# Three pairs of tiles in seven block products instead of two, the first pair's right columns computed last, and the x sums of the second pair made early

## The chip, the cores and the metric

The kernel runs on one core of one Trainium2 chip. The metric is device time in microseconds (us), the median of several executions. One of the executions is recorded by the hardware profiler, and all rows below come from that one. Engines are named as in the profile: PE is TensorE, PEld its weight load, DVE is VectorE, ACT is ScalarE, POOL is GpSimd, SP is SyncE. A small q (SPq, POOLq) means the engine's sequencer: what it does itself, such as issuing DMAs or loading registers.

## The reference

Eight tiles of 128 tokens by 512 features go through a dense layer with one low-rank adapter chosen for each tile, then through a second dense layer with a top-2 gate over eight rank-16 experts. The result is added to x.

```python
A = lora_A[adapter_indices]; Bm = lora_B[adapter_indices]
h = einsum('bsi,io->bso', x, W) + einsum('bsr,bro->bso', einsum('bsi,bir->bsr', x, A), Bm)
result = einsum('bnd,od->bno', h, W_base) + b_base
probs = softmax(einsum('bnd,ed->bne', h, W_gate)); top_p, top_i = top_k(probs, 2)
route_w = sum(one_hot(top_i, E) * (top_p / sum(top_p))[..., None])
delta = einsum('bner,eor->bno', einsum('bnd,erd->bner', h, A_exp) * route_w[..., None], B_exp)
out = x + result + delta
```

## The kernel before

**Fold.** Both dense layers are linear in x, so W is first multiplied into the gate's, the experts' and W_base's columns. This gives one matrix of 648 columns in four row chunks of 128: a left part (8 gate columns, 128 expert columns, 256 output columns, kept in cl_hi and cl_lo with 16 adapter columns beside it, 408 together) and a right part (the other 256 output columns, cr_hi and cr_lo). The identity is added so that x itself comes out too.

**Split in two.** Every fp32 operand is kept as a rounded part (hi) and the remainder (lo), and a `product` (L679 to L682) is three matmuls: hi by hi, hi by lo, lo by hi. ACT makes most hi parts, DVE makes most lo parts by a subtraction (helper `lo`, L500), POOL makes some of both.

**Tiles.** The eight tiles are four pairs q = 0 to 3. Pairs 0 and 3 are computed plainly: `Left(t)` is four products of 408 columns and `Right(t)` four of 256. Pairs 1 and 2 are computed with seven block products (Q1 to Q7, each two chunks deep) in place of eight. Q1, Q2, Q4 and Q5 have 408 columns, Q3, Q6 and Q7 have 256. Q3, Q5, Q6 and Q7 take sums of the two tiles of x, made on POOL by `x_sums` (L324) and split by `split_sums`; Q4 and Q5 take differences of blocks of the folded matrix (u_hi, u_lo), Q6 and Q7 others (v_hi, v_lo), made on DVE and split by ACT and DVE. Between the seven products DVE adds partial results (`sum_v`, `sum_w`, `sum_d`).

**Around the products of a pair.** `split_xa` (DVE) takes the adapter columns out of PSUM, T1 (PE) transposes them, ACT copies them out (`copy_xa_t`), `Lora_left` and `Lora_right` (PE) add the adapter's contribution with rows of bw_rows. bw_rows is filled by DMAs (`spread`) from bw_hi and bw_lo. Then `gate(q)` (DVE, L586) finds the two best experts and writes hw, T2 (PE) transposes hw, ACT and DVE split it (`split_hw`), and `Delta(t)` (PE) adds the experts' part to the left and right output. ACT or DVE copies the outputs to y_out, SP stores them.

**Order.** Each engine's program is one list written by hand, with semaphores between engines. The order of PE is the list from L888 on. POOL's order is: read the adapter numbers into registers (L272), eight DMAs for the adapters' weights (L275), identity and zero fills, the bias rows and their four DMAs (L303), adapter columns of tiles 0 and 1 (`split_la`), then x sums and the rest. SP issues all other loads, then the 24 DMAs of `spread`, then the stores.

Of the kernel before, what the change touches and what calls it, by code (L numbers as in the profile page):

```python
# [5 lines left out]
F32 = mybir.dt.float32  # L6
# [6 lines left out]
NT = 8  # L13
# [13 lines left out]
SEVEN = 2  # L27
LA_ORDER = (0, 1, 2, 3, 4, 5, 6, 7)
# [13 lines left out]
def adaln_ffn_kernel(nc, x_t, itok, fold_in, lora, ffn_b, bias, out):  # L42
    ctx = ExitStack()
    with ctx:
# [3 lines left out]
        def sem(name):  # L48
# [7 lines left out]
        ffn_b_raw = sb("ffn_b_raw", [P, D])  # L56
        bias_raw = sb("bias_raw", [1, D])
# [33 lines left out]
        s_hi, s_lo = (half[:].rearrange("p (n a) (b c x) -> p n (a b) c x", n=SEVEN, b=2, c=2) for half in (wt_hi, wt_lo))  # L91
# [4 lines left out]
        xa_t = sb("xa_t", [P, 2, P], F32R)  # L96
# [21 lines left out]
        left_bank = [(bank[0], bank[1]), (bank[5], bank[2])]  # L118
        right_bank = [(bank[6], bank[7]), (bank[4], bank[3])]
# [18 lines left out]
        last_left_copied = sem("last_left_copied")  # L138
        even_zeros, odd_zeros = sem("even_zeros"), sem("odd_zeros")
        bw_loaded = [sem(f"bw_loaded{q}") for q in range(PAIRS)]  # L140
        bias_rows_loaded = sem("bias_rows_loaded")
# [4 lines left out]
            sem("la_diff_done"), sem("s_summed"), sem("s_hi_done"), sem("s_lo_done"), sem("x_tail_lo_done"))  # L146
        q1_done, q5_done, q6_done, q7_done, q1_copied, v_done, w_done, d_done, yc_done = (
# [38 lines left out]
        def at_front(t):  # L186
            return t in (0, 2, 3, 6)
# [13 lines left out]
        def right(t):  # L201
            return right_whole(t)[:, 0:HALF]

        def t1_out(q):
            return right_whole(2 * q)[:, HALF:HALF + P]

        def t2_out(q):
            return left(4)[:, 0:2 * P] if q == PAIRS - 1 else right_whole(2 * q + 1)[:, HALF:HALF + 2 * P]

        def wait_right_copied(engine, t):  # L210
            if t // 2 in (1, 2):
                engine.wait_ge(yc_done, t - 1)
            else:
                engine.wait_ge(yr_done, t + 1 if t < 2 else t - 3)
# [11 lines left out]

        def sync_program(sp):
# [12 lines left out]
            sp.dma_start(bias_raw[:], bias).then_inc(bias_loaded, DMA)  # L240

            sp.wait_ge(lora_loaded, NT * DMA)
            for t in range(2, NT):
                load_x(t)

            def spread(part, n, q, loaded):
                for h in range(2):
                    sp.dma_start(bw_rows[h * Q + n * R:h * Q + (n + 1) * R, h, q, :].bitcast(F32),
                                 part[h * Q + q * R:h * Q + (q + 1) * R, :].bitcast(F32)).then_inc(loaded, DMA)
# [12 lines left out]

            for t in range(NT - 1):
                sp.wait_ge(yl_done, t + 1)
                wait_right_copied(sp, t)
                sp.dma_start(out[t], y_out[:, t]).then_inc(out_stored, DMA)
            sp.wait_ge(last_left_copied, 1)
            sp.dma_start(out[NT - 1, :, HALF:], y_left(NT - 1)).then_inc(out_stored, DMA)
            sp.wait_ge(out_stored, (NT + 1) * DMA)

        def gpsimd_program(pool):
            _, adapters = nc.values_load_multi_w_load_instructions(  # L272
                itok[0:1, :], engines=[mybir.EngineType.Pool], min_val=0, max_val=NA - 1)
            for b in range(NT):
# [6 lines left out]
            nc.gpsimd.iota(expert_id[:], pattern=[[1, E]], base=0, channel_multiplier=0,  # L281
                           allow_small_or_imprecise_dtypes=True).then_inc(const_ready, 1)

            nc.gpsimd.memset(xa_rows[:].bitcast(F32), 0.0).then_inc(const_ready, 1)
            pool.wait_ge(const_ready, 2)
            for h in range(2):
                nc.gpsimd.memset(xa_rows[:, :, h * Q + ONES:h * Q + ROWS].bitcast(F32), 1.0).then_inc(const_ready, 1)
            pool.wait_ge(const_ready, 4)
            pool.wait_ge(ident_ready, 1)
            nc.gpsimd.tensor_copy(ident_r[:], ident[:]).then_inc(ident_ready, 1)  # L290
            nc.gpsimd.memset(bw_rows[:, 1].bitcast(F32), 0.0).then_inc(odd_zeros, 1)
            pool.wait_ge(odd_zeros, 1)
            pool.wait_ge(even_zeros, 1)

            pool.wait_ge(bias_loaded, DMA)
            nc.gpsimd.tensor_copy(bias_hi[:], bias_raw[:]).then_inc(bias_hi_done, 1)
            pool.wait_ge(bias_hi_done, 1)
            nc.gpsimd.tensor_tensor(bias_lo[:], bias_raw[:], bias_hi[:].bitcast(F32), ALU.subtract).then_inc(bias_lo_done, 1)
            pool.wait_ge(bias_lo_done, 1)
            for h in range(2):  # L300
                for n, part in enumerate((bias_hi, bias_lo)):
                    row = h * Q + ONES + n
                    pool.dma_start(bw_rows[row:row + 1, h, :, GH:].bitcast(F32),  # L303
                                   part[:].bitcast(F32).unsqueeze(1).broadcast_to([1, PAIRS, D])).then_inc(bias_rows_loaded, DMA)

            pool.wait_ge(lora_loaded, NT * DMA)

            def split_la(t):
                n = LA_ORDER.index(t)
                odd = t in (3, 5)  # L310
                if t in (2, 4, 6, 7):
                    pool.wait_ge(left_done, {2: 1, 4: 2, 6: 3, 7: 5}[t])
# [11 lines left out]
            def x_sums(q):  # L324
                n = q - 1
                a, b = x_raw[:, 2 * q], x_raw[:, 2 * q + 1]
                pool.wait_ge(cl_lo_done, 1)
                pool.wait_ge(x_loaded[2 * q], DMA)
                pool.wait_ge(x_loaded[2 * q + 1], DMA)
                nc.gpsimd.tensor_tensor(s_raw[n][0][:, 0], b[:, 0:2], b[:, 2:4], ALU.add).then_inc(s_summed, 1)  # L330
                pool.wait_ge(s_summed, 4 * n + 1)
                nc.gpsimd.tensor_tensor(s_raw[n][0][:, 1], s_raw[n][0][:, 0], a[:, 0:2], ALU.add).then_inc(s_summed, 1)
                pool.wait_ge(s_summed, 4 * n + 2)
                nc.gpsimd.tensor_tensor(s_raw[n][1][:, 0], s_raw[n][0][:, 1], a[:, 2:4], ALU.add).then_inc(s_summed, 1)
                nc.gpsimd.tensor_tensor(s_raw[n][1][:, 1], a[:, 0:2], b[:, 0:2], ALU.add).then_inc(s_summed, 1)

            def split_sums(q, h):
# [15 lines left out]
            split_sums(2, 0)  # L353
            split_la(4)
            split_la(5)
            split_sums(2, 1)
            pool.wait_ge(hw_done, 4)
            for t in (NT - 2, NT - 1):
                pool.wait_ge(x_hi_done, t + 1)
                nc.gpsimd.tensor_tensor(x_lo[:, t], x_raw[:, t], x_hi[:, t].bitcast(F32), ALU.subtract).then_inc(x_tail_lo_done, 1)  # L360
            split_la(6)
            split_la(7)

        def scalar_program(act):
# [14 lines left out]
            def split_x(t):  # L379
                chunks = slice(2, KC) if t in (3, 5) else slice(0, KC)  # L380
# [3 lines left out]
            split_x(0)  # L384
            split_x(1)
# [3 lines left out]
            act.wait_ge(ffn_b_loaded, DMA)  # L389
            nc.scalar.copy(ffn_b_hi[:], ffn_b_raw[:]).then_inc(ffn_b_hi_done, 1)  # L390
# [6 lines left out]
            for n in range(2):  # L397
                act.wait_ge(cr_summed, n + 1)
                if n == 0:
                    act.wait_ge(cr_plus_i, 1)  # L400
                nc.scalar.copy(cr_hi[:, 2 * n:2 * n + 2, :].rearrange("p c n -> p (c n)"), bank[4 + n][:]).then_inc(cr_hi_done, 1)
# [584 lines left out]
```

## Time and profile before

| what | value |
|---|---|
| runs | 64.83, 65.61 and 66.38 us, median 65.61 us |
| profiled execution, its own time | 64.86 us |
| its span, first to last instruction | 63.6 us |
| PE busy | 59.8 us, 94% of the span |
| DVE, POOL, ACT busy | 42.0, 31.5, 29.9 us |
| granted TensorE clock | 1.000 throughout |

A row of the timeline gives the start, the duration, engine, line, operation, output and inputs, and how often it stands in the row. PE's matmuls are pipelined: the step from the start of one to the start of the next is what one costs, the duration also holds the way through the array. A bracket gives the idle time just before a row and what ended it.

### The profile page before, as it was taken

How to read it: one execution, taken by the hardware profiler on the slowest of the kernel's cores; microseconds unless marked ns; L12 is line 12 of the kernel's file. 1: busy time of each engine (PE TensorE's matmuls, PEld its weight loads, DVE VectorE, ACT ScalarE, POOL GpSimd, SP SyncE). 2: the span in 40 equal slices, each digit the busy share in tenths (PEclk: the TensorE clock that was granted, in tenths of full speed). 3: DMA queues.
4: the chain of work that ended last, by engine and by line, in shares of the span. 5: the costliest groups of instructions: out<-in, count | busy, mean ns of one | idle time of the engine just before them, and what ended most of it. 6: DMA issues, size and time to landing. Idle time of an engine off the chain costs nothing.

```text
span 63.6 us, 1254 instructions
## 1 busy us (share of the span) xinstructions
PE 59.8 (94%) x406; PEld 58.8 (92%) x406; DVE 42.0 (66%) x129; ACT 29.9 (47%) x69; POOL 31.5 (49%) x58
## 2 busy tenths in 40 slices
PE   4979999999999999999999999999999999999930
PEld 4969999999999999999999999999999999999820
DVE  0948799918089789999798489089373774195220
ACT  1753999334349869777455014580224102422240
POOL 1000799899969899999865891005960000000000
PEclk9999999999999999999999999999999999999999
DMA  0799999506796000323232323171003400000827
GB/s 0 195 394 345 378 391 406 205 15 184 254 315 255 7 0 0 72 59 72 59 73 62 75 55 84 28 271 67 0 0 148 182 0 10 0 0 13 317 90 240
DMA packets 5048, 8.46 MB, mean 133 GB/s; under 512 B 1057, under 2 KB 1569, under 8 KB 5042
## 3 DMA queue, kind: packets, MB, share of 16 engines
q1 hardware_dynamic: 4370, 7.57, 36.5%
q0 software_dynamic: 384, 0.56, 2.5%
q10 hardware_dynamic: 288, 0.27, 1.2%
q8 instruction: 3, 0.05, 0.3%
q14 instruction: 3, 0.02, 0.1%
HBM read 5.26 MB, written 2.10 MB: 116 GB/s over the span
## 4 chain that ended last, share of the span: by engine, by line
PE 90%; DMA 5%; ACT 1%; issue 0%
PE bank L680 22%; PE bank L682 21%; PE bank L681 21%; PE bank L688 8%; PE bank L690 6%; DMA w_raw<-fold_in 5%; PE bank L843 3%; PE bank L805 2%; PE bank L813 1%; PE bank L847 1%; PE bank L822 1%; ACT y_out L446 1%; PE bank L858 1%; PE bank L854 1%; PE bank L794 0%
## 5 line engine op out<-in xcount | busy, mean ns | idle before, releaser
L680 PE MATMUL bank<-cl_hi,x_hi 128*128 128x408 f32 x24 | 8.5, 356 | 0.0
L682 PE MATMUL bank<-cl_hi,x_lo 128*128 128x408 f32 x24 | 8.4, 348 | 0.0
L681 PE MATMUL bank<-cl_lo,x_hi 128*128 128x408 f32 x24 | 8.3, 348 | 0.0
L275 POOL DMA_DIRECT2D lora_raw<-lora x8 | 4.5, 564 | 6.4 <-issue 6.2
L341 POOL TENSOR_TENSOR wt_lo<-w_raw,wt_hi 128x512 fp32r<-128x512 f32 x4 | 5.5, 1383 | 1.6 <-DVE hw L605 1.3
L438 ACT CAST hw_hi<-bank 128x256 fp32r<-128x256 f32 x4 | 1.5, 373 | 9.1 <-PE bank L822 9.1
L442 ACT COPY y_out<-bank 128x256 f32<-128x256 f32 x7 | 2.6, 374 | 5.3 <-PE bank L682 5.2
L360 POOL TENSOR_TENSOR x_lo<-x_raw,x_hi 128x512 fp32r<-128x512 f32 x2 | 2.5, 1294 | 5.1 <-DVE hw L605 5.1
L501 DVE TENSOR_TENSOR x_lo<-x_raw,x_hi 128x512 fp32r<-128x512 f32 (+1 forms) x6 | 4.9, 834 | 0.0
L680 PE MATMUL bank<-ffn_b_hi,hw_hi 128*128 128x256 f32 x16 | 4.8, 297 | 0.0
L680 PE MATMUL bank<-cr_hi,x_hi 128*128 128x256 f32 x16 | 4.6, 290 | 0.0
L681 PE MATMUL bank<-ffn_b_lo,hw_hi 128*128 128x256 f32 x16 | 4.5, 284 | 0.0
L681 PEld LDWEIGHTS bank<-cl_lo,x_hi 128*128 128x128 f32 x24 | 4.5, 189 | 0.0
L680 PEld LDWEIGHTS bank<-cl_hi,x_hi 128*128 128x128 f32 x24 | 4.5, 188 | 0.0
L682 PE MATMUL bank<-ffn_b_hi,hw_lo 128*128 128x256 f32 x16 | 4.5, 282 | 0.0
L681 PE MATMUL bank<-cr_lo,x_hi 128*128 128x256 f32 x16 | 4.5, 282 | 0.0
L682 PE MATMUL bank<-cr_hi,x_lo 128*128 128x256 f32 x16 | 4.5, 282 | 0.0
L682 PEld LDWEIGHTS bank<-cl_hi,x_lo 128*128 128x128 f32 x24 | 4.5, 188 | 0.0
L382 ACT CAST x_hi<-x_raw 128x512 fp32r<-128x512 f32 (+1 forms) x8 | 4.2, 566 | 0.0
L680 PE MATMUL bank<-wg_hi,wt_hi 128*128 128x392 f32 (+2 forms) x12 | 3.9, 326 | 0.0
L681 PE MATMUL bank<-wg_lo,wt_hi 128*128 128x392 f32 (+2 forms) x12 | 3.9, 324 | 0.0
L682 PE MATMUL bank<-wg_hi,wt_lo 128*128 128x392 f32 (+2 forms) x12 | 3.9, 324 | 0.0
(151 smaller groups left out, 197.3 us busy)
## 6 DMA issues: line engine op xcount, KB each, us to landing
x_raw<-x_t SPq DMA_DIRECT2D x8, 256.0 KB, 4.6
out<-y_out SPq DMA_DIRECT2D x7, 256.0 KB, 2.1
w_raw<-fold_in SPq DMA_DIRECT2D x4, 256.0 KB, 4.7
w_raw<-fold_in SPq DMA_DIRECT2D x3, 324.0 KB, 4.8
bw_rows<-bw_hi SPq DMA_DIRECT2D x16, 40.5 KB, 2.0
lora_raw<-lora POOLq DMA_DIRECT2D x8, 64.0 KB, 3.2
bw_rows<-bw_lo SPq DMA_DIRECT2D x8, 40.5 KB, 2.1
ffn_b_raw<-ffn_b SPq DMA_DIRECT2D x1, 256.0 KB, 6.0
```

The costliest lines, as they stand in the source:

```text
L275: pool.dma_start(lora_raw[:, b, :], lora[bass.ds(adapters[b], 1), :, :].rearrange("a p c -> (a p) c")).then_inc(lora_loaded, DMA)
L341: nc.gpsimd.tensor_tensor(s_lo[:, n, two], s_raw[n][h], s_hi[:, n, two].bitcast(F32), ALU.subtract).then_inc(s_lo_done, 1)
L360: nc.gpsimd.tensor_tensor(x_lo[:, t], x_raw[:, t], x_hi[:, t].bitcast(F32), ALU.subtract).then_inc(x_tail_lo_done, 1)
L382: nc.scalar.copy(x_hi[:, t, chunks], x_raw[:, t, chunks]).then_inc(x_hi_done, 1)
L442: nc.scalar.copy(y_left(t), left(t)[:, OUT_LEFT]).then_inc(yl_done, 1)
L501: nc.vector.tensor_tensor(out, raw, hi.bitcast(F32), ALU.subtract).then_inc(done, 1)
L680: nc.tensor.matmul(out, a_hi, b_hi, start=first, stop=False, skip_group_check=True)
L681: nc.tensor.matmul(out, a_hi, b_lo, start=False, stop=False, skip_group_check=True)
L682: return nc.tensor.matmul(out, a_lo, b_hi, start=False, stop=last, skip_group_check=True)
L688: nc.tensor.matmul(bank[i][:, cols], w[:, m, rows], wg[:, m, cols], start=False, stop=False, skip_group_check=True)
L690: nc.tensor.matmul(fold_right(i), w[:, m, rows], wg[:, m, LEFT:], start=False, stop=False, skip_group_check=True)
L843: nc.tensor.matmul(bank[i][:, 0:GH], w_raw[:, 0, i * P:(i + 1) * P], raw_gh(0), start=True, stop=False, skip_group_check=True)
```

## The change

Pair 3 is computed with Q1 to Q7 as well. The right columns of tiles 0 and 1 (`Right(0)`, `Right(1)`) leave the beginning of PE's tile list and stand behind pair 3's delta, with `Lora_right(0)` and the right deltas of tiles 0 and 1; both results share one PSUM bank and leave by one copy and one store. `Delta` is divided into a left and a right part. Left banks of tiles 2, 3 and the right bank of tile 1's old place are exchanged (PSUM banks 2, 5, 7).

The x sums of pair 1 move on POOL from behind the adapter columns to in front of them, right behind the identity, with their own tiles s_first; their lo part moves from POOL to DVE. POOL now also makes ffn_b_lo, cr_lo of the last two chunks, and the x sums of pair 3. The four bias DMAs move from POOL to SP. The two DMAs of bw_lo for pair 0 move from SP to POOL. POOL's two long fills (bw_rows, xa_rows) move in front of the register loads. SP loads x of tiles 2 and 3 before ffn_b. On DVE the lo parts of v stand in front of the adapter columns of tiles 0 and 1. At the end ACT stores the left half of tile 7 and SP the right half.

```diff
-            load_x(0)
-            load_x(1)
-            sp.dma_start(ffn_b_raw[:], ffn_b).then_inc(ffn_b_loaded, DMA)
+            for t in range(4):
+                load_x(t)
...
             sp.wait_ge(lora_loaded, NT * DMA)
+            sp.dma_start(ffn_b_raw, ffn_b).then_inc(ffn_b_loaded, DMA)
...
         def gpsimd_program(pool):
+            nc.gpsimd.memset(bw_rows[:, 1].bitcast(F32), 0.0).then_inc(odd_zeros, 1)
+            nc.gpsimd.memset(xa_rows[:].bitcast(F32), 0.0).then_inc(const_ready, 1)
             _, adapters = nc.values_load_multi_w_load_instructions(
...
+            x_sums(1)
+            nc.gpsimd.iota(expert_id[:], pattern=[[1, E]], base=0, channel_multiplier=0,
...
             split_la(0)
             split_la(1)
-            x_sums(1)
...
+            pool.wait_ge(ffn_b_hi_done, 1)
+            nc.gpsimd.tensor_tensor(ffn_b_lo[:], ffn_b_raw, ffn_b_hi[:].bitcast(F32), ALU.subtract).then_inc(ffn_b_lo_done, 1)
             x_sums(2)
+            pool.wait_ge(cr_tail_hi_done, 1)
+            nc.gpsimd.tensor_tensor(cr_lo[:, 2:4], cr_raw, cr_hi[:, 2:4].bitcast(F32), ALU.subtract).then_inc(cr_tail_lo_done, 1)
+            pool.wait_ge(bw_lo_done, 2)
+            pool.wait_ge(even_zeros, 1)
+            pool.wait_ge(odd_zeros, 1)
+            spread(pool, bw_lo, 1, 0, first_bw_lo_loaded)
             split_la(2)
-            split_sums(1, 0)
             split_la(3)
-            split_sums(1, 1)
+            x_sums(3)
             pool.wait_ge(hw_done, 2)
...
+            for h in range(2):
+                dve.wait_ge(s_hi_done, h + 1)
+                two = slice(2 * h, 2 * h + 2)
+                lo(s_part(1, 1)[:, two], s_raw[0][h], s_part(0, 1)[:, two], first_s_lo_done)
...
-            ALL = (0, 1, 2, 3)
-            Left(0, ALL)
-            Left(1, ALL)
-            Right(0, ALL)
+            Left(0)
+            Left(1)
+            Q6(1)
             T1(0)
-            Right(1, ALL)
+            Q1(1)
             Lora_left(0)
-            Lora_right(0)
-
-            Q1(1)
-            Q6(1)
             Q5(1)
             Q7(1)
             Q2(1)
             T2(0)
+            Q3(1)
             Q4(1)
-            Q3(1)
-            Delta(0)
-            Delta(1)
+            Delta_left(0)
+            Delta_left(1)
             T1(1)
...
-            Left(6, (0, 1))
+            Q1(3)
             Lora_left(2)
-            Left(6, (2, 3))
-            Left(7, (0, 1, 2))
+            Q6(3)
+            Lora_right(2)
+            Q5(3)
+            Q7(3)
+            Q2(3)
             T2(2)
-            Left(7, (3,))
-            Q3(2)
-            Lora_right(2)
+            Q4(3)
+            Q3(3)
             T1(3)
-            Delta(4)
+            Delta_left(4)
+            Delta_right(4)
             Lora_left(3)
-            Delta(5)
-            Right(6, ALL)
-            Right(7, (0, 1))
+            Delta_left(5)
+            Delta_right(5)
+            Right(0, (0, 1, 2, 3))
+            Right(1, (0, 1))
             T2(3)
-            Right(7, (2, 3))
+            Right(1, (2, 3))
+            Lora_right(0)
+            Delta_right(0)
+            Delta_right(1)
             Lora_right(3)
-            Delta(6)
-            Delta(7)
+            for t in (6, 7):
+                Delta_left(t)
+                Delta_right(t)
```

## Rows read from the trace of the kernel before

**Rows 1.** The page, busy time of each engine and its share of the span.
```profile
PE 59.8 (94%) x406; PEld 58.8 (92%) x406; DVE 42.0 (66%) x129; ACT 29.9 (47%) x69; POOL 31.5 (49%) x58
```
**Rows 2.** Busy time by stretch: length, PE, PEld, DVE, ACT, POOL, clock, DMA.
```profile
27.73:39.60 11.87, 11.87 (x87) 11.82 (x87) 10.11 (x32) 5.67 (x15) 8.65 (x15) 1.00 0.31 67
61.10:63.60 2.50, 0.00 (x0) 0.00 (x0) 0.05 (x1) 0.36 (x1) 0.00 (x0) 1.00 0.60 210
```
**Rows 3.** The page, the chain that ended last, shares of the span by engine.
```profile
PE 90%; DMA 5%; ACT 1%; issue 0%
```
**Rows 4.** Timeline of PE, from Lora_left(0) to Delta(0).
```profile
30.69 0.52 PE L805 MATMUL bank<-bw_rows,xa_t 114*128 114x392 f32 x2
31.05 0.41 PE L813 MATMUL bank<-bw_rows,xa_t 114*128 114x256 f32 x2
31.30 0.35 PE L680 MATMUL bank<-cl_hi,x_hi 128*128 128x408 f32 x1
...
32.42 0.28 PE L680 MATMUL bank<-v_hi,wt_hi 128*128 128x256 f32 x1
...
37.40 0.28 PE L680 MATMUL bank<-cr_hi,wt_hi 128*128 128x256 f32 x1
...
38.11 0.28 PE L680 MATMUL bank<-ffn_b_hi,hw_hi 128*128 128x256 f32 x1
```
**Rows 5.** Timeline of PE, the last Lora_right and the first matmul of Delta(6).
```profile
58.98 0.40 PE L813 MATMUL bank<-bw_rows,xa_t 114*128 114x256 f32 x2
59.35 0.38 PE L680 MATMUL bank<-ffn_b_hi,hw_hi 128*128 128x256 f32 x1
```
**Rows 6.** Timeline of ACT and of DVE, the last copies to y_out.
```profile
61.09 0.37 ACT L446 COPY y_out<-bank 128x256 f32<-128x256 f32 x1 [0.34 <-PE bank L682]
...
60.73 0.42 DVE L676 COPY y_out<-bank 128x256 f32<-128x256 f32 x1 [1.43 <-PE bank L682]
```
**Rows 7.** Timeline of POOL: set-up, bias, adapter columns, x sums, a lo part.
```profile
12.29 0.13 POOL L281 IOTA expert_id<- 128x8 f32 x1
...
13.16 2.27 POOL L291 MEMSET bw_rows<- 128x2592 f32 x1
...
17.90 0.52 POOL L303 DMA_DIRECT2D bw_rows<-bias_hi  x1 [0.29 <-POOL bias_lo L298]
...
20.24 0.25 POOL L318 CAST cl_hi<-lora_raw 128x64 fp32r<-128x64 f32 x1
...
21.68 0.74 POOL L330 TENSOR_TENSOR w_raw<-x_raw 128x256 f32<-128x256 f32 x1
...
24.72 0.73 POOL L330 TENSOR_TENSOR w_raw<-x_raw 128x256 f32<-128x256 f32 x1
25.53 1.13 POOL L332 TENSOR_TENSOR w_raw<-w_raw,x_raw 128x256 f32<-128x256 f32 x1
...
31.56 1.30 POOL L341 TENSOR_TENSOR wt_lo<-w_raw,wt_hi 128x512 fp32r<-128x512 f32 x1
```
**Rows 8.** Timeline of DVE: a lo part of x, gate(0), its sums, gate(1)'s onehot.
```profile
25.38 0.68 DVE L501 TENSOR_TENSOR x_lo<-x_raw,x_hi 128x512 fp32r<-128x512 f32 x1
...
31.25 0.17 DVE L588 MAX8 top_val<-bank 128x8 f32<-128x8 f32 x1 [0.31 <-PE bank L805]
...
32.02 0.88 DVE L594 TENSOR_TENSOR onehot<-expert_id,top_idx 128x32 f32<-128x32 f32 x1
...
33.51 0.61 DVE L605 SCALAR_TENSOR_TENSOR hw<-bank,top_rcp,route 128x128 f32<-128x128 f32 x2
...
35.15 0.43 DVE L622 TENSOR_TENSOR bank<-bank,w_raw 128x256 f32<-128x256 f32 x1 [0.21 <-PE bank L682]
...
42.11 0.19 DVE L594 TENSOR_TENSOR onehot<-expert_id,top_idx 128x32 f32<-128x32 f32 x1
```
**Rows 9.** POOL's sequencer: the loads of the adapter numbers (duration, first and last start).
```profile
L272 POOLq TENSOR_LOAD <-itok x1: 2412/2412/2412, 1.7 to 1.7; - x1
```
**Rows 10.** The page, DMA issues: KB each, us from issue to landing.
```profile
ffn_b_raw<-ffn_b SPq DMA_DIRECT2D x1, 256.0 KB, 6.0
```

More of the change, by code:

```diff
@@ L225, in adaln_ffn_kernel, with spread @@
         LORA_LEFT = slice(R, OWN)
+        def spread(engine, part, n, q, loaded):
+            for h in range(2):
+                engine.dma_start(bw_rows[h * Q + n * R:h * Q + (n + 1) * R, h, q, :].bitcast(F32),
+                                 part[h * Q + q * R:h * Q + (q + 1) * R, :].bitcast(F32)).then_inc(loaded, DMA)
         def sync_program(sp):
@@ L244, in sync_program @@
+            for t in range(4, NT):
                 load_x(t)
[L246 to L249, printed above, removed]
             sp.wait_ge(even_zeros, 1)
             sp.wait_ge(odd_zeros, 1)
+            sp.wait_ge(bias_lo_done, 1)
+            for h in range(2):
+                for n, part in enumerate((bias_hi, bias_lo)):
+                    row = h * Q + ONES + n
+                    sp.dma_start(bw_rows[row:row + 1, h, :, GH:].bitcast(F32),
+                                 part[:].bitcast(F32).unsqueeze(1).broadcast_to([1, PAIRS, D])).then_inc(bias_rows_loaded, DMA)
@@ L263, in sync_program @@
-            for t in range(NT - 1):
+                spread(sp, bw_hi, 0, q, bw_loaded[q])
+                spread(sp, bw_hi, 2, q, bw_loaded[q])
+                spread(sp, bw_lo, 1, q, bw_loaded[q])
+            sp.wait_ge(yl_done, 2)
+            sp.dma_start(out[0:2, :, HALF:].rearrange("t p d -> p t d"), y_out[:, 0:2, HALF:]).then_inc(out_stored, DMA)
+            for t in range(2, 6):
                 sp.wait_ge(yl_done, t + 1)
-                wait_right_copied(sp, t)
+                sp.wait_ge(yc_done, t - 1)
@@ L280, in gpsimd_program @@
                                     pattern=[[-1, P]], channel_multiplier=1).then_inc(ident_ready, 1)
[L281 to L306, printed above, removed]
             def split_la(t):
                 n = LA_ORDER.index(t)
-                odd = t in (3, 5)
+                odd = t in (3, 5, 7)
                 if t in (2, 4, 6, 7):
-                    pool.wait_ge(left_done, {2: 1, 4: 2, 6: 3, 7: 5}[t])
+                    pool.wait_ge(left_done, {2: 1, 4: 2, 6: 3, 7: 4}[t])
                 hi, lo = (u_hi, u_lo) if odd else (cl_hi, cl_lo)
@@ L396, in scalar_program @@
                 nc.scalar.copy(cl_hi[:, i, LORA_LEFT], bank[i][:, 0:LEFT]).then_inc(cl_hi_done, 1)
[L397 to L401, printed above, removed]
+                if i == 1:
+                    act.wait_ge(ffn_b_loaded, DMA)
+                    nc.scalar.copy(ffn_b_hi[:], ffn_b_raw).then_inc(ffn_b_hi_done, 1)
+            act.wait_ge(cr_plus_i, 1)
+            nc.scalar.copy(cr_hi[:, 0:2, :].rearrange("p c n -> p (c n)"), bank[4][:]).then_inc(cr_hi_done, 1)
             for i in range(2):
@@ L523, in vector_program @@
                 lo(lb(lb_lo, h), raw_lb(h), lb(lb_hi, h), lb_lo_done)
-            dve.wait_ge(ffn_b_hi_done, 1)
-            lo(ffn_b_lo[:], ffn_b_raw[:], ffn_b_hi[:], ffn_b_lo_done)
+            for h in range(2):
+                dve.wait_ge(s_hi_done, h + 1)
+                two = slice(2 * h, 2 * h + 2)
+                lo(s_part(1, 1)[:, two], s_raw[0][h], s_part(0, 1)[:, two], first_s_lo_done)
             def split_left(i):
@@ L549, in vector_program @@
             split_left(3)
-            for n in range(2):
-                split_right(n)
+            dve.wait_ge(cr_hi_done, 1)
+            lo(cr_lo[:, 0:2, :].rearrange("p c n -> p (c n)"), bank[4][:], cr_hi[:, 0:2, :].rearrange("p c n -> p (c n)"), cr_lo_done)
             dve.wait_ge(c_raw_done, 3)
@@ L673, in vector_program @@
             split_hw(3)
[L675 to L676 removed]
+            out_right(6)
+            out_right(7)
         def tensor_program(pe):
```

320 lines of the change are left out of this document (173 added, 147 removed).

## Prediction

> **What bounds the kernel now.** I read the page's busy table first: PE has 59.8 us of 63.6, nearly its whole span, and POOL, which this change loads more, 31.5 [rows 1]. The chain that ended last is 90% PE and 5% DMA, the loads before PE's first matmul and the last store [rows 3]. So PE is not only busy, it is the chain. The stretches then say whether it ever waits: from 27.73, where Right(0) begins, to 39.60 it is busy 11.87 us of 11.87, and in the last 2.50 us it does nothing, as only copies and stores are left [rows 2]. Two things can therefore move the end: the number of matmuls, or a wait that PE does not have today. The timelines of the other engines show how early each of PE's inputs is ready.
>
> **What PE saves.** Plain pair 3 takes 8 products of 408 columns and 8 of 256. In seven products it takes 8 of 408 (Q1, Q2, Q4, Q5, two chunks each) and 6 of 256. Two products of 256 go, six matmuls. Q3(1) is six such matmuls and takes 38.11 - 37.40 = 0.71 us [rows 4]. All other work on PE keeps its count. So -0.7.
>
> A small wait goes too. The last Lora_right ends its issue at 58.98 + 0.24, but Delta(6) starts at 59.35 and its first matmul takes 0.38 us instead of 0.28, as hw_lo has only just come [rows 5, 4]. After the change 1.9 us of matmuls that need nothing of gate 3 stand between T2(3) and that delta (half of Right(1), two Lora_right, two right deltas: 6 + 2 + 6 + 2 matmuls at about 0.12). So -0.2. Together -0.9.
>
> **The end.** Before, the last copy is ACT's, 0.37 us from 61.09; now it is DVE's out_right, and a DVE copy of that size took 0.42 [rows 6]. The last stretch stays DMA-bound at a busy share of 0.60 [rows 2]. The store of the first pair's right halves falls in front of it, but can be issued some 1.0 us before PE ends (Lora_right(3) and the last deltas are 14 matmuls, 1.7 us, less the copy). I take 0, bounds -0.1 and +0.4.
>
> **What moves to the front on PE.** Right(0) and Right(1) covered 24 matmuls, 2.9 us, between the fold and pair 1. Everything that pair 1 needs is due that much earlier. Steps: a Q of 408 columns costs 32.42 - 31.30 = 1.12, one of 256 costs 0.71, Lora_left 0.36 [rows 4]. Left(1) still ends at 27.73. Then Q6(1) to 28.44, T1(0), Q1(1) from 28.5 to 29.6, Lora_left(0) at 29.6 (before: 30.69), Q5, Q7, Q2, and T2(0) at 32.9.
>
> **POOL, in front of Q1(1).** Q1(1) needs tile 2's adapter columns, split_la(2), now the end of a long POOL list. It starts when x of tile 3 has landed: ffn_b, issued third behind x, took 6.0 us and would be in by about 11.8 [rows 10]; x of tile 3 comes one transfer of 256 KB later, about 12.4 (estimate). Prices [rows 7]: x_sums 24.72 - 21.68 = 3.04, twice; the small set-up 13.16 - 12.29 less the fill that left, 0.6; split_la (21.68 - 20.24)/2 = 0.72, three times; bias from 15.43 (end of the fill) to 17.90, 2.4; ffn_b_lo and the rest of cr_lo 1.30 each; two DMA issues (20.24 - 17.90)/2 = 1.2. Sum 15.0, so split_la(2) ends at 27.4, and Q1(1) wants it at 28.5. 1.1 us to spare, if nothing slows POOL.
>
> Something does. At 25.53 an x sum took 1.13 us instead of 0.74, beside a DVE subtraction with both inputs in SBUF from 25.38 to 26.06: 0.39 lost [rows 7, 8]. Before the change the x sums of pair 1 had no such neighbours. Now seven DVE subtractions of this kind come beside POOL's list: x of tiles 2 and 3, the two lb_lo, the two lo parts of the first x sums, and the first of v. None hitting costs 0, all cost 2.7; I take half, 1.35, as each can also be the one that waits. POOL then ends at 28.75 and Q1(1) waits 0.25 (bounds 0 and 1.6). bw_lo's DMAs, moved to POOL's queue just ahead, are issued 0.72 before split_la(2) ends and due at Lora_left(0), 1.1 behind Q1(1)'s start; these 1.8 us cover the transfer, and without that cover it adds to the same wait. The wait for bw_lo on POOL is over by then; queued behind it are split_la(2), split_la(3) and x_sums(3).
>
> The Trainium skill, page "SBUF — State Buffer", section "SBUF: two separate sides", gives a rule for this: DVE, with two SBUF inputs, and a POOL instruction reading SBUF take an exclusive lock, and the loser waits for the whole instruction. The rows agree in kind (0.39 of 0.68 lost after a start 0.15 later). By the rule all seven meetings would cost in full; that is the second rival.
>
> **DVE, in front of T2(0).** gate(0) started 0.56 us after Lora_left(0) and had hw at 34.12, 2.87 later. Of this 0.69 is a meeting: onehot took 0.88 and ended at 32.90, beside a POOL subtraction from 31.56 to 32.86; gate(1)'s took 0.19 [rows 4, 7, 8]. Free, hw comes 0.56 + 2.18 = 2.74 after Lora_left(0), and T2(0) now wants it after 3.29 (0.36 + 1.12 + 0.71 + 1.12): 0.55 to spare. sum_d ends 1.46 after hw (35.58 - 34.12), 0.21 of that a wait, so at 3.99, and Q4(1) wants it at 4.2 (T2 about 0.2 and Q3 0.71 later): 0.2 to spare. But x_sums(3) now stands on POOL just there: from about 29.8 to 32.8 (split_la(3) about 1.0, then 3.04) against gate(0) at 30.4. I take one meeting at the row's price, 0.69, less the 0.2: 0.5. Bounds 0 and 1.3 (gate held until x_sums(3) is over).
>
> **Edits that I cost at nothing.** POOL's fills in front of the register loads: the loads run on POOL's sequencer (2.4 us for the numbers alone) while the engine idles [rows 9], so 2.6 us of fill hide there; without that cover see the third rival. The bias DMAs on SP stand in its wait for bw_hi. The two DMAs fewer of pair 0 bring all later spreads forward. v's lo parts stand in front on DVE, where the lo parts of x 2 and 3 stood; I count them as in time for Q6(1) at 27.7, and if they are late, that goes into the same 0.25 and its bounds, since Q1(1) stands right behind. The exchanged banks and new slots add waits that are long met. T1(1), T1(3) and Q1(2) have only about 0.1 to 0.2 us to spare; whatever delays DVE shows there next.
>
> **Sum.** -0.7 - 0.2 + 0.25 + 0.5 = -0.15. On the profiled execution's own 64.86 us this gives 64.7. That execution stands 0.75 under the median of the runs, near the lowest; a median should come at 65.61 - 0.15 = 65.5 us.
>
> **Rivals.**
> - *POOL keeps up.* Meetings on POOL cost under 1.1 and gate(0) slips between the x sums. Then no new wait: -0.9, 64.7 as a median. For it: 1.1 us of slack, and that each meeting has two possible losers. Against: onehot's 0.88. Chance 0.33.
> - *POOL late in full, slower than before.* All seven meetings cost 0.39: split_la(2) ends at 30.1, Q1(1) waits 1.6; x_sums(3) runs to 34.2 and holds gate(0) until then; from the end of onehot hw took 34.12 - 32.90 = 1.2, so hw is at 35.4 against 33.95 free, 1.45 late, 1.25 behind the slack of Q4. 2.85 - 0.9 = +1.95, median 67.55. It decides for "slower" as soon as both waits pass 2.2. For it: POOL and DVE are both nearly full in that stretch (8.65 and 10.11 us of 11.87 even before [rows 2]). Against: in the rows not every meeting cost POOL. Chance 0.20.
> - *The fills delay the register loads.* If POOL's sequencer waited for its engine, the adapter DMAs and all of POOL's list come 2.6 us later: Q1(1) waits 2.85, net +2.45, median 68.05. Against: nothing is waited for between fill and loads. Chance 0.06.
>
> The forecast, a part of the saving eaten by one or both waits, has 0.37; its own range is 64.9 to 66.6 (net -0.7 to +1.0). 0.04 is left for a wait that I have not seen.
>
> **Range.** The first rival, at 64.7 with 0.4 for the spread of the runs, sets the low end, 64.3; the second, half of it, the high end, 67.3. About 2% is what a measurement of this kernel can tell from no change: 64.3 and 66.9. Faster by more needs 1.3 us, and only 0.9 is to be saved, so 0.05 (spread alone). Slower: most of the second rival, the third, a little of the rest, 0.25. Within: 0.70.
>
> **What would show it.** PE's busy time falls by about 0.7 and its idle time shows a wait in front of Q1(1) put down to POOL's split_la(2) (L320), and one in front of T2(0) or Q4(1) put down to DVE. x_sums rows above 0.74 us beside DVE's lo rows confirm the meetings; gate(0)'s onehot or top_diff above 0.2 the second wait. The adapter DMAs on POOL must not start later than before. The prediction is wrong if PE has no idle time (first rival), if the adapter DMAs start some 2.6 us later (third), or if the end is not 2.5 us after PE's last matmul.

## The result, and the profile after

The changed kernel takes 65.95 us in the median, the kernel before 64.77 in the runs beside it. The ratio is 1.020, with a 95% interval of 1.0155 to 1.0242. So the change makes the kernel about 2% slower, at least 1.5% by the interval. Ratios compare runs in the faster of the two states that executions fall into, so they can differ from the ratio of two medians. I had forecast a net of -0.15 us, next to no change. The profiled execution takes 65.83 us with a span of 64.6, which is 1.0 more than before, at a granted clock of 1.00 throughout.

First the page of the changed kernel: the busy table, and of the chain that ended last the shares by engine.

```profile
PE 59.8 (92%) x400; PEld 58.1 (90%) x400; DVE 44.4 (69%) x133; ACT 30.8 (48%) x70; POOL 36.9 (57%) x63
...
PE 84%; DVE 5%; DMA 5%; issue 2%
```

Six matmuls are gone (400 for 406 in [rows 1]), and still PE is as long busy as before. The reason comes below: a short wait in front of a matmul is covered by the listed duration of the matmul before it, and so shows as busy time. The chain was 90% PE [rows 3]. Now it is 84%, and DVE stands in it with 5%, where it did not appear before. POOL has 5.4 us more to do.

Next the busy time by stretch of the changed kernel (length, then PE, PEld, DVE, ACT, POOL, clock, DMA).

```profile
27.73:36.00 8.27, 7.24 (x42) 6.21 (x42) 6.63 (x25) 4.12 (x10) 6.61 (x13) 1.00 0.34 76
36.00:45.00 9.00, 9.00 (x60) 8.94 (x60) 5.49 (x25) 2.67 (x8) 6.42 (x11) 1.00 0.20 55
...
62.00:64.60 2.60, 0.00 (x0) 0.00 (x0) 0.42 (x1) 0.05 (x1) 0.00 (x0) 1.00 0.83 290
```

Before, PE was busy every moment from 27.73 to 39.60 [rows 2]. Now it loses 1.03 us of busy time in the first 8.27 us and nothing from 36 to 45. The last stretch is about as long as before (2.60 for 2.50), and fuller of transfers (0.83 for 0.60). The timeline of PE in the changed kernel shows the places.

```profile
28.25 0.26 PE L817 MATMUL bank<-ident_r,xa_rows 128*114 128x128 f32 x1
29.18 0.42 PE L704 MATMUL bank<-cl_hi,x_hi 128*128 128x408 f32 x1 [0.66 <-issue]
...
30.36 0.54 PE L829 MATMUL bank<-bw_rows,xa_t 114*128 114x392 f32 x2
...
33.48 0.34 PE L706 MATMUL bank<-cl_hi,x_lo 128*128 128x408 f32 x1
34.09 0.59 PE L844 MATMUL bank<-ident,hw 128*128 128x128 f32 x2 [0.26 <-DVE hw L628]
34.67 0.39 PE L704 MATMUL bank<-cr_hi,s_first_hi 128*128 128x256 f32 x1
...
35.38 0.28 PE L706 MATMUL bank<-cr_hi,s_first_lo 128*128 128x256 f32 x1
35.76 0.43 PE L704 MATMUL bank<-wg_hi,x_hi 128*128 128x408 f32 x1
```

Read the starts, not the durations. T1(0) starts at 28.25 and Q1(1) only at 29.18; where nothing waits that step is 0.10, so 0.83 is lost. The last matmul of Q2 starts at 33.48 and costs 0.19, so T2(0) was due at 33.67. It starts at 34.09, and Q3 behind it starts 0.58 later, where that step takes 0.13 in a kernel without the wait: T2's second transpose waits for its own half of hw, and Q3 waits for DVE's next sum, `sum_v`. Q4(1) starts 0.38 behind the last matmul of Q3 instead of 0.11; it waits for the last of these sums, `sum_d`. The bracket in front of Q1(1) names no releaser ("issue"); what it waited for is seen in POOL's timeline of the changed kernel.

```profile
12.95 1.07 POOL L335 TENSOR_TENSOR w_raw<-x_raw 128x256 f32<-128x256 f32 x1 [0.67 <-DMA x_raw<-x_t]
14.09 0.80 POOL L337 TENSOR_TENSOR w_raw<-w_raw,x_raw 128x256 f32<-128x256 f32 x1
...
16.94 0.68 POOL L363 CAST ident_r<-ident 128x128 fp32r<-128x128 f32 x1
17.57 0.70 POOL L318 CAST cl_hi<-lora_raw 128x64 fp32r<-128x64 f32 x1
...
25.00 1.20 POOL L340 TENSOR_TENSOR w_raw<-x_raw 128x256 f32<-128x256 f32 x1
...
28.76 0.32 POOL L320 TENSOR_TENSOR cl_lo<-lora_raw,cl_hi 128x64 fp32r<-128x64 f32 x1
...
31.01 0.73 POOL L337 TENSOR_TENSOR w_raw<-w_raw,x_raw 128x256 f32<-128x256 f32 x1
31.83 0.74 POOL L339 TENSOR_TENSOR w_raw<-w_raw,x_raw 128x256 f32<-128x256 f32 x1
32.52 0.74 POOL L340 TENSOR_TENSOR w_raw<-x_raw 128x256 f32<-128x256 f32 x1
```

split_la(2) ends at 29.08, and Q1(1) starts 0.10 later. The x sums that took 0.74 in [rows 7] take up to 1.20. Then gate(0), `sum_v` (L635) and `sum_d` (L645) in DVE's timeline of the changed kernel.

```profile
31.22 0.55 DVE L613 TENSOR_TENSOR top_diff<-top_val 128x4 f32<-128x4 f32 x1
...
32.09 0.52 DVE L617 TENSOR_TENSOR onehot<-expert_id,top_idx 128x32 f32<-128x32 f32 x1
32.64 0.63 DVE L620 TENSOR_TENSOR top_sum<-top_exp 128x2 f32<-128x2 f32 x1
...
33.68 0.61 DVE L628 SCALAR_TENSOR_TENSOR hw<-bank,top_rcp,route 128x128 f32<-128x128 f32 x2
34.20 0.41 DVE L635 TENSOR_TENSOR w_raw<-bank,w_raw 128x256 f32<-128x256 f32 x1
...
35.18 0.43 DVE L645 TENSOR_TENSOR bank<-bank,w_raw 128x256 f32<-128x256 f32 x1
```

Three subtractions and sums on a handful of elements take 0.52 to 0.63. gate(1)'s onehot took 0.19 [rows 8]. Set the two fences side by side: top_diff ends at 31.77 and the x sum beside it at 31.74; onehot at 32.61 and 32.57; top_sum at 33.27 and 33.26. Each DVE instruction ends as soon as the POOL instruction that was running when it began is over. The row of before that the prediction leaned on shows the same: onehot ended at 32.90, the POOL subtraction beside it at 32.86 [rows 7, 8].

The Trainium skill, page "SBUF — State Buffer", section "SBUF: two separate sides", states such a lock: a DVE instruction with two SBUF inputs and a GpSimd instruction that reads SBUF exclude each other for a whole instruction, and the one that starts first goes first. These three pairs of ends agree with it within 0.04 us. The 0.16 to 0.19 us that these instructions take when nothing holds them do not come on top.

### The profile page after: what moved, and what is told of

It reads as the page before. It is cut to its first block, busy times and chain, and to the rows that moved or that the text cites. A ratio compares the mean times of both kernels' runs of the same rounds, so it can differ in the third digit from the quotient of the medians.

```text
span 64.6 us, 1257 instructions
## 1 busy us (share of the span) xinstructions
PE 59.8 (92%) x400; PEld 58.1 (90%) x400; DVE 44.4 (69%) x133; ACT 30.8 (48%) x70; POOL 36.9 (57%) x63
## 4 chain that ended last, share of the span: by engine, by line
PE 84%; DVE 5%; DMA 5%; issue 2%
PE bank L704 21%; PE bank L706 19%; PE bank L705 19%; PE bank L712 8%; PE bank L714 5%; DMA w_raw<-fold_in 5%; PE bank L869 3%; PE bank L829 2%; PE bank L844 2%; PE bank L835 1%; PE bank L873 1%; DVE top_sum L620 1%; DVE top_diff L613 1%; DVE onehot L617 1%; DVE y_out L649 1%
## 5 line engine op out<-in xcount | busy, mean ns | idle before, releaser
L704 PE MATMUL bank<-cl_hi,x_hi 128*128 128x408 f32 x20 | 7.1, 354 | 0.7 <-issue 0.7
L705 PE MATMUL bank<-cl_lo,x_hi 128*128 128x408 f32 x20 | 7.0, 348 | 0.0
L706 PE MATMUL bank<-cl_hi,x_lo 128*128 128x408 f32 x20 | 7.0, 348 | 0.0
L704 PEld LDWEIGHTS bank<-cl_hi,x_hi 128*128 128x128 f32 x20 | 3.8, 188 | 0.8 <-issue 0.8
L649 DVE TENSOR_TENSOR y_out<-bank,w_raw 128x256 f32<-128x256 f32 x6 | 2.4, 421 | 2.7 <-PE bank L706 2.7
L526 DVE TENSOR_TENSOR x_lo<-x_raw,x_hi 128x512 fp32r<-128x512 f32 (+1 forms) x6 | 3.9, 709 | 0.0
L705 PEld LDWEIGHTS bank<-cl_lo,x_hi 128*128 128x128 f32 x20 | 3.8, 188 | 0.0
L706 PEld LDWEIGHTS bank<-cl_hi,x_lo 128*128 128x128 f32 x20 | 3.8, 188 | 0.0
L402 ACT CAST wt_hi<-w_raw 128x512 fp32r<-128x512 f32 x4 | 2.5, 620 | 2.6 <-DMA w_raw<-fold_in 2.4
L863 PE MATMUL bank<-const-bfloat16-1.0 128*128 128x128 bf16 x24 | 2.7, 309 | 0.9 <-PEq L1011 0.9
```

The costliest lines, as they stand in the source:

```text
L526: nc.vector.tensor_tensor(out, raw, hi.bitcast(F32), ALU.subtract).then_inc(done, 1)
L649: nc.vector.tensor_tensor(y_right(t), right(t), w_sum[:, (t // 2 - 1) % 2], ALU.add if t % 2 else ALU.subtract).then_inc(yc_done, 1)
L704: nc.tensor.matmul(out, a_hi, b_hi, start=first, stop=False, skip_group_check=True)
L705: nc.tensor.matmul(out, a_hi, b_lo, start=False, stop=False, skip_group_check=True)
L706: return nc.tensor.matmul(out, a_lo, b_hi, start=False, stop=last, skip_group_check=True)
L863: nc.tensor.matmul(bwr_bank[:, 0:P], ones, ones, start=True, stop=True)
```

## The experiments

The theory after this reading: the saving on PE is there in full, and two waits eat it, both made of meetings between POOL instructions and DVE subtractions. Runs are compared with the kernel before on the same chip. Start times vary between executions even for the same code (in the traces below the fold begins between 5.58 and 7.45), so beside the medians I use the distance from the first split matmul of the fold to the last matmul of the kernel. It is 54.06 us before (6.71 to 60.77) and 55.23 after (6.48 to 61.71). One thing it does not take out: where Q1(1) waits for POOL, it starts when POOL's list ends, whenever the fold began, so an early fold makes that wait longer and the distance with it. Free of this is the stretch from Q1(1)'s start to the last matmul, 32.53 after (29.18 to 61.71).

**Without the x sums of the second block pair.**

```diff
             split_la(3)
-            x_sums(3)
...
-                act.wait_ge(s_summed, 4 * n + 2 * h + 2)
+                act.wait_ge(s_summed, min(4 * n + 2 * h + 2, 8))
```

> The changed kernel without POOL's four x sums of pair 3 (left out of the computation: pair 3 takes the old sums of pair 1). In the changed kernel gate(0) takes 3.36 us from its first MAX8 to the end of hw, against 2.18 free, and PE waits about 0.85 at T2(0) and 0.26 at Q4(1). Theory (the x sums of pair 3 stand beside gate(0) and hold its subtractions and products with two SBUF inputs): gate(0) goes back to 2.2 us, both waits at T2(0) and Q4(1) go, the wait of 0.87 in front of Q1(1) stays, the time falls by about 1.1 us. Rival (without Right(0) and Right(1) in front, the way from Lora_left(0) over gate(0) to T2(0) and Q4(1) is too long whatever POOL does): PE still waits over 0.6 us there and the time falls by less than 0.4.

Measured: 64.83 us, ratio 1.0048 (1.0005 to 1.0091). The distance is 53.93, 1.30 less than after. gate(0) takes 2.18 from MAX8 to the end of hw, as it does in the kernel before without the meeting, and T2(0) and Q4(1) wait for nothing. The wait in front of Q1(1) is still there (0.5). So the second wait is x_sums(3). Not all of the 1.30 is its price: split_la(2) ends at 29.04 here, as in the changed kernel (29.08), but the fold begins 0.28 later, so 0.3 is a shorter wait in front of Q1(1). From Q1(1)'s start (29.14) on it is 31.55, 0.98 less than after, and some 0.2 of that stretch is lost at Lora_left(0), which starts 0.33 behind the last matmul of Q1 where it takes 0.18 in the changed kernel. bw_lo's two DMAs took 2.4 us to land here and 2.1 there; whether that is the reason is not shown. So x_sums(3) costs about 1.2.

**POOL's list in front of split_la(2) shortened by one entry.**

```diff
-            pool.wait_ge(ffn_b_hi_done, 1)
-            nc.gpsimd.tensor_tensor(ffn_b_lo[:], ffn_b_raw, ffn_b_hi[:].bitcast(F32), ALU.subtract).then_inc(ffn_b_lo_done, 1)
...
             split_la(3)
+            pool.wait_ge(ffn_b_hi_done, 1)
+            nc.gpsimd.tensor_tensor(ffn_b_lo[:], ffn_b_raw, ffn_b_hi[:].bitcast(F32), ALU.subtract).then_inc(ffn_b_lo_done, 1)
             x_sums(3)
```

> The changed kernel with one POOL instruction moved: the lo part of ffn_b (1.29 us) stands behind split_la(3) in place of in front of the second x sums. Theory (two waits in a row): split_la(2) ends near 27.8 in place of 29.1, so the wait of 0.87 in front of Q1(1) goes; but the x sums of pair 3 still end near 33.3 and hold gate(0) until then, so hw comes no earlier, the waits at T2(0) and Q4(1) grow by 0.8 to 0.9, and the time stays within 0.3 us of the changed kernel. Rival (the two waits are independent): the time falls by 0.8 to 0.9 us.

Measured: 65.48 us, ratio 1.0111 (1.0066 to 1.0157); distance 54.45, 0.78 less than after. Q1(1) now starts without a wait, so it was POOL's list that held it. The kernel gains nearly all of that wait. The three meetings of gate(0) remain (top_diff 0.59, onehot 0.52, top_sum 0.62), with the same waits at T2(0) and Q4(1) behind them: gate(0) begins 0.62 earlier, the x sums 0.59. My theory, that a gain in front of Q1(1) would largely be lost again at T2(0), was too pessimistic; the medians (0.47) lie between the two expectations, the distances at the rival's.

**Both edits.**

> Both edits together: the lo part of ffn_b late on POOL, and POOL's x sums of pair 3 left out of the computation. Theory: no wait is left on PE, the time falls by 1.9 to 2.1 us against the changed kernel, to about 1 us below the kernel before: the six matmuls (0.7) and the wait at Delta(6) (0.2) show. Rival (pair 1 is simply too early in PE's list, and each wait removed is followed by the next): it falls by less than 1.3 us and stays at or above the kernel before.

Measured: 64.29 us, ratio 0.9944 (0.99 to 0.9988); distance 53.19. The busy time by stretch of this kernel (columns as above), then PE's timeline at Q1(1) and at the last matmul:

```profile
27.73:36.00 8.27, 8.27 (x55) 8.21 (x54) 6.30 (x30) 4.66 (x13) 4.82 (x7) 1.00 0.31 67
```
```profile
28.83 0.40 PE L703 MATMUL bank<-cl_hi,x_hi 128*128 128x408 f32 x1
...
60.15 0.28 PE L705 MATMUL bank<-ffn_b_hi,hw_lo 128*128 128x256 f32 x1
```

PE waits nowhere behind the fold. Against the kernel before the distance is 0.87 shorter, the -0.9 that the prediction gave PE. The medians show less of it: 64.29 is 1.66 below the changed kernel's 65.95, not 1.9 to 2.1, and 0.41 below the 64.70 of before, not about 1. From Q1(1)'s start on, the two kernels with x_sums(3) take 32.53 and 32.58, this one 31.32: x_sums(3) costs 1.21 to 1.26. By the distances the first edit is worth 1.30 alone and 1.26 with the other, the second 0.78 alone and 0.74 with the other; that these agree so closely is partly chance, as the fold's start is in them.

**Is it POOL's being busy, or its reading SBUF?** Fills of the same length in place of the x sums.

```diff
+                if q == 3:
+                    for i in range(4):
+                        if i >= 2:
+                            pool.wait_ge(s_summed, 4 * n + i - 1)
+                        free = y_out[:, 2 + 2 * (i % 2):4 + 2 * (i % 2)].rearrange("p t d -> p (t d)")
+                        nc.gpsimd.memset(free[:, 0:850], 0.5).then_inc(s_summed, 1)
+                    return
```

> The changed kernel with four fills of 850 columns on POOL (about 0.75 us each, into an unused part of y_out) in place of the four x sums of pair 3 (left out of the computation). They keep POOL busy in the same stretch for as long, but read nothing from SBUF. Theory (only POOL instructions that read SBUF hold back DVE's instructions with two SBUF inputs): top_diff, onehot and top_sum of gate(0) take 0.16 to 0.2 us each, gate(0) 2.2 us, the time is that of the kernel without the sums. Rival (any POOL instruction at work there holds gate(0)): they take 0.4 to 0.7 us as in the changed kernel and gate(0) over 3 us.

DVE's timeline of this kernel, in gate(0):

```profile
31.25 0.17 DVE L620 TENSOR_TENSOR top_diff<-top_val 128x4 f32<-128x4 f32 x1
...
31.74 0.19 DVE L624 TENSOR_TENSOR onehot<-expert_id,top_idx 128x32 f32<-128x32 f32 x1
31.97 0.16 DVE L627 TENSOR_TENSOR top_sum<-top_exp 128x2 f32<-128x2 f32 x1
```

And POOL's timeline of this kernel beside it, all four fills in one row:

```profile
30.19 3.06 POOL L340 MEMSET y_out<- 128x850 f32 x4
```

POOL is busy from 30.19 to 33.25, as long and at the same time as with the x sums, and gate(0) is free. So it was not POOL's being busy that held DVE. A fill differs from an x sum in reading nothing from SBUF, which is the theory's point; it is also another operation, and no run sets the two apart. (One execution, 64.64 us. Its fold began 0.9 earlier and its PE waited as much longer for POOL in front of Q1(1), so its time says little; the rows of gate(0) are the result.)

**The first wait without the meetings.** The DVE subtractions beside POOL's list become fills of the same outputs, so the list itself is unchanged.

```diff
+                if t in (2, 3):
+                    nc.vector.memset(x_lo[:, t, chunks].bitcast(F32), 0.0).then_inc(x_lo_done, 1)
+                    return
...
-                lo(lb(lb_lo, h), raw_lb(h), lb(lb_hi, h), lb_lo_done)
+                nc.vector.memset(lb(lb_lo, h).bitcast(F32), 0.0).then_inc(lb_lo_done, 1)
...
-                lo(s_part(1, 1)[:, two], s_raw[0][h], s_part(0, 1)[:, two], first_s_lo_done)
+                nc.vector.memset(s_part(1, 1)[:, two].bitcast(F32), 0.0).then_inc(first_s_lo_done, 1)
...
-            lo(v_lo[:, 0:2], c_raw[:, :, GH:], v_hi[:, 0:2], t_lo_done)
+            nc.vector.memset(v_lo[:, 0:2].bitcast(F32), 0.0).then_inc(t_lo_done, 1)
```

> Seven DVE subtractions with two inputs in SBUF that stand beside POOL's list (lo parts of x of tiles 2 and 3, both of lb_lo, both of the first x sums, the first of v) are replaced by fills with zero of the same outputs, so these lo parts are left out of the computation. Theory (POOL is late at split_la(2) because its instructions and DVE's subtractions hold each other up): POOL's rows fall back to 0.74 for an x sum, 0.29 for ident_r, 0.24 for la's hi part, 0.6 for bias_hi stays or falls, split_la(2) ends 1 to 2 us earlier than 29.08, and no wait stands before Q1(1); the waits at T2(0) and Q4(1) stay unless x_sums(3), moved earlier by as much, clears gate(0): by 1.9 us earlier it would run 28.3 to 31.3 and still meet MAX8's successors at 31. Time 64.9 to 65.2. Rival (the list is simply too long and starts too late): the rows stay near the after ones, split_la(2) ends within 0.5 us of 29.08, and the wait at Q1(1) stays above 0.4 us.

POOL's timeline of this kernel, at the rows that were shown of the changed kernel:

```profile
12.87 0.74 POOL L335 TENSOR_TENSOR w_raw<-x_raw 128x256 f32<-128x256 f32 x1 [0.15 <-DMA x_raw<-x_t]
13.69 0.75 POOL L337 TENSOR_TENSOR w_raw<-w_raw,x_raw 128x256 f32<-128x256 f32 x1
...
16.30 0.29 POOL L363 CAST ident_r<-ident 128x128 fp32r<-128x128 f32 x1
16.53 0.24 POOL L318 CAST cl_hi<-lora_raw 128x64 fp32r<-128x64 f32 x1
...
23.45 0.74 POOL L340 TENSOR_TENSOR w_raw<-x_raw 128x256 f32<-128x256 f32 x1
...
26.75 0.32 POOL L320 TENSOR_TENSOR cl_lo<-lora_raw,cl_hi 128x64 fp32r<-128x64 f32 x1
```

The same list takes 14.20 us (12.87 to 27.07) instead of 16.13 (12.95 to 29.08). The seven meetings cost POOL 1.93, and without them Q1(1) does not wait. One expectation missed: I thought that gate(0) would still meet x_sums(3). As PE did not wait, gate(0) began at 30.22 and x_sums(3) ended at 31.27; only onehot was caught (0.33 for 0.19), and these 0.14 are all that PE still waits, at Q4(1). The distance is 53.28 and the time 64.06 us (one execution), under the 64.9 that I had expected. Both waits go back to the same seven meetings: they make POOL late, and POOL's lateness puts x_sums(3) where gate(0) runs.

**The cover put back.** Useless matmuls where Right(0) and Right(1) stood.

```diff
+            pe.wait_ge(bw_lo_done, 2)
+            pe.wait_ge(cr_lo_done, 1)
+            for _ in range(17):
+                nc.tensor.matmul(bank[6][:, 0:HALF], x_hi[:, 0, 0, :], cr_hi[:, 0, :], start=True, stop=True, skip_group_check=True)
```

> The changed kernel with 17 matmuls of 256 columns whose results are not used put between Left(1) and Q6(1), where Right(0) and Right(1) stood before: about 17 x 0.119 = 2.0 us of cover. Theory (the change lost because it took away the cover in front of pair 1, and what it waits for there is due 2.9 us earlier): the waits before Q1(1), T2(0) and Q4(1), 2.05 us in all, nearly vanish, and the time is within 0.5 us of the changed kernel's, ratio to before 1.015 to 1.03. Rival (the waits come from an order in which PE's own matmuls release POOL or DVE, so that they move along with PE): the time is longer than the changed kernel's by about 2 us, ratio 1.045 to 1.055.

Measured: 66.00 us, ratio 1.0196 (1.0093 to 1.03), no different from the changed kernel. The distance is 55.62, so 2.0 us of added work cost 0.4. The waits in front of Q1(1) and T2(0) are gone, and behind T2(0) some 0.45 us stay: Q3 starts 0.30 behind T2(0) for 0.13, and Q4(1) 0.39 behind Q3's last matmul for 0.11. In this run one x sum still stands beside gate(0), for one meeting (top_diff takes 0.64 for 0.16). The waits do not move along with PE's order: the time of POOL and DVE was always needed, and Right(0) and Right(1) had hidden it.

**A version that keeps the saving.** ffn_b_lo stands behind split_la(3), and DVE makes these x sums itself, in its idle time in front of gate(1); ACT's and POOL's splits of them move behind that. Nothing is left out.

```diff
-            x_sums(3)
...
+            plus_1, plus_2 = s_raw[0]
+            a, b = x_raw[:, 6], x_raw[:, 7]
...
+            nc.vector.tensor_tensor(plus_1[:, 0], b[:, 0:2], b[:, 2:4], ALU.add).then_inc(s_summed, 1)
+            dve.wait_ge(s_summed, 9)
+            nc.vector.tensor_tensor(plus_1[:, 1], plus_1[:, 0], a[:, 0:2], ALU.add).then_inc(s_summed, 1)
+            dve.wait_ge(s_summed, 10)
+            nc.vector.tensor_tensor(plus_2[:, 0], plus_1[:, 1], a[:, 2:4], ALU.add).then_inc(s_summed, 1)
+            nc.vector.tensor_tensor(plus_2[:, 1], a[:, 0:2], b[:, 0:2], ALU.add).then_inc(s_summed, 1)
```

> The changed kernel with both waits of its front taken away and nothing left out: ffn_b_lo behind split_la(3) on POOL, and the x sums of the second pair's tiles made by DVE itself in its idle time between split_x(5) and gate(1), with their splits on ACT and POOL moved behind them. Theory (the two waits are all that the change costs): as with x_sums(3) left out and ffn_b_lo moved, PE has no wait from 27.7 us on, gate(0) takes about 2.2 us from MAX8 to hw, and the time is about 64.3 us, ratio to the kernel before 0.985 to 0.998. Rival: the four sums (about 0.6 to 0.9 us each) on DVE make gate(1) late at T2(1), or their splits make Q6(3) late, a new wait of 0.3 to 1 us, and the time is 64.7 us or more. A second rival, that POOL needs the time of x_sums(3) for nothing and the change is still slower by something else, would show as idle time of PE elsewhere.

Measured: 64.15 us, ratio to the kernel before 0.9939 (0.989 to 0.9989). DVE's timeline of this kernel has the first and the last of the four sums, and gate(1) right behind.

```profile
37.62 0.45 DVE L681 TENSOR_TENSOR w_raw<-x_raw 128x256 f32<-128x256 f32 x1
...
38.91 0.42 DVE L686 TENSOR_TENSOR w_raw<-x_raw 128x256 f32<-128x256 f32 x1
39.34 0.17 DVE L610 MAX8 top_val<-bank 128x8 f32<-128x8 f32 x1
```

And the busy time by stretch of this kernel (columns as above), where the changed kernel had its waits and where the sums now lie:

```profile
27.73:36.00 8.27, 8.27 (x54) 8.21 (x53) 6.26 (x28) 3.91 (x10) 4.71 (x8) 1.00 0.33 72
36.00:45.00 9.00, 9.00 (x63) 8.95 (x62) 7.18 (x30) 3.78 (x11) 5.13 (x11) 1.00 0.24 63
```

PE has no wait left; from Q1(1)'s start to the last matmul it takes 31.29. The sums take 0.42 to 0.45 each on DVE, against 0.74 on POOL, and gate(1) is not made late. This is faster than both kernels, against the kernel before by 0.6%, a small gain whose interval reaches from 0.1% to 1.1%.

## Why the prediction was wrong, point by point

The span gives the balance, in the prediction's own terms. The run with both edits stands for a changed kernel without waits:

| term | predicted | measured | from |
|---|---|---|---|
| six matmuls and the wait at Delta(6) | -0.9 | -0.87 | both edits, less before |
| wait in front of Q1(1) | +0.25 | +0.78 | after, less ffn_b_lo late |
| gate(0) beside x_sums(3) | +0.5 | +1.26 | ffn_b_lo late, less both edits |
| the end | 0 | +0.06 | last matmul's start to the end of the span: 2.83, 2.89 |
| the start of the fold | none | -0.23 | 6.71, 6.48 |
| sum | -0.15 | +1.00 | spans 63.6, 64.6 |

The rows of Q1(1) and of the fold's start belong together: POOL's list sets when Q1(1) starts, so a fold that begins 0.23 earlier only waits 0.23 longer. Counted from the fold of before, the wait in front of Q1(1) is 0.55 (0.78 - 0.23) against the predicted 0.25, and the one at gate(0) is the larger miss.

**Right.** What bounds the kernel, what PE saves, the end, and the places, names and causes of both waits. Lora_left to T2(0) was to be 3.29 (the four terms written beside it add up to 3.31) and is 3.30 with both edits; gate(0) was to start 0.56 behind Lora_left(0) and starts 0.57 behind it (30.36, 30.93); free it takes 2.18. bw_lo's DMAs on POOL caused no wait in the changed kernel. The adapter DMAs start at 6.87 (before 6.81), so the fills in front of the register loads cost nothing, as I had taken it, and the third rival falls. One of the signs did not come: PE's busy time was to fall by 0.7 and stayed at 59.8, because part of its waiting is listed as busy.

**Wrong: "I take half, 1.35".** This is the step that failed first. The meetings cost POOL 1.93 of the 2.7 that all seven could. Two other errors on that line cancel in part (+0.55 and -0.80): POOL's list begins at 12.95, not at 12.4, as x of tile 3 landed later than I estimated, and without meetings it takes 14.20, not 15.0 (I had set the bias at 2.4 and the two DMA issues at 1.2; they are 1.93 and 1.02). So split_la(2) ends at 29.08, 0.33 later than the predicted 28.75. Q1(1) was due at 28.35, 0.15 earlier than I said, as the fold of this execution began early, and starts 0.10 after split_la(2) ends. 0.25 + 0.33 + 0.15 + 0.10 = 0.83, the wait in the trace.

**Wrong: "I take one meeting at the row's price, 0.69, less the 0.2".** This term was off by more. I saw that x_sums(3) stands beside gate(0), and then priced it as one meeting because the trace of before had shown one. But x_sums(3) is four reading instructions back to back, for 3.1 us, and gate(0) has three two-input instructions of SBUF in that time; each of them meets one. The price of one is not 0.69, it is what is left of the POOL instruction: 0.39, 0.33 and 0.47, together 1.19. And the slack of 0.2 was not there. Q4(1) starts 0.15 after sum_d's end (35.61 and 35.76), a handover that I left out, and with both edits, where nothing is late, sum_d ends at 34.08 and Q4(1) starts at 34.23, just when it is due. So the 1.19 shows in full: it is 1.21 to 1.26 in the stretch behind Q1(1)'s start. The run without the seven meetings says the same: one meeting of 0.14, and 0.14 of wait at Q4(1).

**Wrong: no sum for what the cover had been worth.** I listed what becomes due 2.9 us earlier and gave each item its slack. On POOL's list and on gate(0)'s way these slacks were 0.2 to 1.1 us, and two engines fuller than before had to meet them. My second rival, POOL late in full, +1.95, was nearer (+1.2 in the medians): its price for gate(0) was 1.25, measured 1.26, and only its wait at Q1(1), 1.6, was too high. By the rows alone it deserved more than the 0.20 that I gave it.

**The base.** I added 0.75 us because the profiled execution stood under the median of three runs. In larger groups of runs the kernel before has medians of 64.77, 64.70 and 65.09, so the profiled 64.86 was an ordinary one, and most of the 0.75 was scatter. That the forecast of 65.5 lies near 65.95 is luck, two errors of opposite sign: +0.84 in the base (65.61 for 64.77) and -1.33 in the change (-0.15 for +1.18). The range's high end does not come out as written either: half of the second rival's 1.95 on 65.6, with the same 0.4 for the spread, is 67.0 and not 67.3.

## What to carry to other kernels

Where PE is the chain, work that stands early and is needed late is cover; before it is moved to the end, add up what the other engines must deliver in that time, on the fuller engines. Wherever POOL reads SBUF back to back, count every DVE instruction with two SBUF inputs that falls beside it as held until the running POOL instruction ends, and the POOL instructions as held in their turn. A small chain on DVE that PE waits for (a gate) should have no such neighbour; a sum that takes DVE 0.43 in an idle stretch is cheaper there than 0.74 on POOL beside a gate.

## What the runs showed of the hardware

- POOL's casts, with one SBUF input, are held as well: ident_r took 0.68 for 0.29, the first hi part of the adapter columns 0.70 for 0.24. POOL's fills, which read nothing, did not hold gate(0) (3.06 us of fills beside it, and its instructions as short as when free).
- T2(0)'s two matmuls are shown as busy without a gap, for 0.59 in the changed kernel, where the second waits and Q3 behind it too, and for 0.38 in the last version. Comparing starts finds such waits, PE's busy time hides them.
- From PE's first matmul on loaded data to the first split matmul passed 1.71 us in one run (the one with fills, 3.87 to 5.58), 2.57 in the changed kernel (3.91 to 6.48) and 3.33 in the last version (4.12 to 7.45), at a granted clock of 1.00 and with the same code there. PE shows no wait in it; the matmuls themselves follow at another pace. Those of 136 columns are listed with 0.434 us each in the last version and start 0.23 apart, and with 0.279 in the run with fills, where they start 0.12 apart. What sets the pace was not tried and stays open. The spread is as large as the effect of the change, and may be part of why the medians alone do not show the sum above.
